# Context keys and values of two heads computed in the first stages and fetched in the attention

## The reference

```python
x = _layernorm(x + _L0_attn_ref(x, w1, w2, b2, sparse_mask))          # dense, masked, gelu
x = _layernorm(x + _L0_xattn_ref(x, ctx_4096, ctx_4096))              # autocorrelation
x = _layernorm(x + _L0_ffn_ref(x, base_W, router_W, lora_A, lora_B))  # routed low-rank
x = _layernorm(x + _L1_attn_ref(x, in_proj_w, ...))                   # state-space mixer
x = _layernorm(x + _L1_xattn_ref(x, ctx_4096, Wq, Wk, Wv, Wo, ...))   # cross attention
x = _layernorm(x + _L1_ffn_ref(x, gate, kernel, ...))                 # adapters
# in _L1_xattn_ref, with 32 query heads and 8 key heads of 128:
kv = jnp.concatenate([context, latents], axis=1)     # 128 context and 128 latent tokens
k = (kv @ Wk) ; v = (kv @ Wv)                        # then rms_norm of q and k, softmax, @ v, @ Wo
```

## Time and profile before

| | |
|---|---|
| median of 3 runs | 2551.83 us (2551.8 to 2552.94) |
| profiled execution, its own time | 2551.84 us |
| its span | 2550.1 us |
| TensorE busy | 2477.9 us, 97% |
| VectorE busy | 1866.3 us, 73% |
| ScalarE busy | 1122.6 us, 44% |
| GpSimd busy | 1082.3 us, 42% |

### The profile page before, as it was taken

The page is one execution under the profiler, slowest core; times in us unless marked ns, Lnnn a source line. Parts: engine busy times, 40 slices in busy tenths (PEclk is TensorE's granted clock), DMA queues, the critical chain, the costliest instruction groups (busy, mean ns, idle before and its releaser), DMA issues. The chain is left out here.

```text
span 2550.1 us, 39113 instructions
## 1 busy us (share of the span) xinstructions
PE 2477.9 (97%) x14056; PEld 2033.2 (80%) x14056; DVE 1866.3 (73%) x2530; ACT 1122.6 (44%) x2660; POOL 1082.3 (42%) x890
## 2 busy tenths in 40 slices
PE   7989899999999999999999999899999999999999
PEld 4547788888888888888888887788888888888886
DVE  4877986886977968859869678656666666666675
ACT  2323343343443443433434433455656556555551
POOL 3012655645655655556566555632312223222123
PEclk8999999999999999999999999999999999999999
DMA  4000420321412303313213131110101001000100
GB/s 151 28 1 9 164 101 30 144 95 54 145 42 91 120 29 120 116 38 136 71 64 139 38 116 64 60 42 26 34 18 34 26 17 42 16 27 26 56 3 34
DMA packets 61554, 163.82 MB, mean 64 GB/s; under 512 B 8336, under 2 KB 8976, under 8 KB 52944
## 3 DMA queue, kind: packets, MB, share of 16 engines
q1 hardware_dynamic: 60144, 159.21, 18.2%
q10 hardware_dynamic: 1248, 2.36, 0.3%
HBM read 158.92 MB, written 2.62 MB: 63 GB/s over the span
## 5 line engine op out<-in xcount | busy, mean ns | idle before, releaser
L271 PE MATMUL pair<-XH,d_w_hi 128*128 128x512 f32 x1160 | 471.8, 407 | 2.8 <-DVE d_gated L1633 1.7
L272 PE MATMUL pair<-XL,d_w_hi 128*128 128x512 f32 x1160 | 460.3, 397 | 0.0
L273 PE MATMUL pair<-XH,d_w_lo 128*128 128x512 f32 x1160 | 459.7, 396 | 0.0
L1492 POOL TENSOR_TENSOR d_decay<-d_decay,d_cb 128x1024 f32<-128x1024 f32 x128 | 311.1, 2431 | 137.2 <-DVE d_decay L1610 137.2
L1610 DVE TENSOR_TENSOR_SCAN d_decay<-d_decay,m_delta 128x1024 f32<-128x1024 f32 x128 | 363.5, 2841 | 1.5 <-DVE d_dtg L1578 1.5
L1473 POOL TENSOR_TENSOR d_w_lo<-d_w,d_w_hi 128x512 fp32r<-128x512 f32 x144 | 188.6, 1312 | 268.1 <-ACT d_w_hi L1313 267.4
L271 PEld LDWEIGHTS pair<-XH,d_w_hi 128*128 128x128 f32 x1160 | 218.8, 189 | 60.1 <-issue 12.8
L1595 DVE SCALAR_TENSOR_TENSOR d_hs<-pair,d_conv,d_hs 128x1016 f32<-128x1016 f32 (+2 forms) x192 | 242.9, 1265 | 29.2 <-ACT d_hs L1338 24.7
L273 PEld LDWEIGHTS pair<-XH,d_w_lo 128*128 128x128 f32 x1160 | 218.7, 189 | 52.9
L272 PEld LDWEIGHTS pair<-XL,d_w_hi 128*128 128x128 f32 x1160 | 219.0, 189 | 47.1
L1497 POOL TENSOR_TENSOR d_gated_lo<-d_gated,d_gated_hi 128x512 fp32r<-128x512 f32 x128 | 173.4, 1357 | 159.1 <-ACT d_gated_hi L1357 159.1
(11 more groups left out here) (280 smaller groups left out, 6032.4 us busy)
## 6 DMA issues: line engine op xcount, KB each, us to landing
d_decay<-token_decays SPq DMA_DIRECT2D x64, 1024.0 KB, 4.9
d_w<-in_L_w_groups SPq DMA_DIRECT2D x144, 256.0 KB, 2.7
e_w<-in_L_w_heads SPq DMA_DIRECT2D x80, 256.0 KB, 2.7
d_wo<-in_L_wo_groups SPq DMA_DIRECT2D x64, 256.0 KB, 4.9
X<-in_x SPq DMA_DIRECT2D x8, 256.0 KB, 10.3
b_ctx<-in_ctx SPq DMA_DIRECT2D x8, 256.0 KB, 12.0
e_ctx<-in_ctx_t SPq DMA_DIRECT2D x4, 512.0 KB, 6.5
out<-X SPq DMA_DIRECT2D x8, 256.0 KB, 2.0
```

Source lines behind the costliest of these rows:

```text
L271: pe.matmul(out, wh, xh, start=first, stop=False)
L272: pe.matmul(out, wh, xl, start=False, stop=False)
L273: return pe.matmul(out, wl, xh, start=False, stop=last)
L1492: pool.tensor_tensor(r, r, GM_[:], ALU.mult).then_inc(q["scores"], 1)
```

## The change

A new class `KeysAhead` projects the context's keys and values of heads 2 and 5 before the attention, as eight items of two batches (24 matmuls of 256 columns each). Items 0 and 1 stand behind the last dense batch in block one, in banks 4 and 5; items 2 to 7 stand in the autocorrelation, in bank 3 that its correlation also uses: item 2 ahead of `spectra(2)`, items 3 to 7 around `turn_weights` of batches 0, 2, 3, 4 and 5, half before and half after. For that the context and the weights are fetched and split in block one (residuals of batches 4 to 7, and the weights of the second head, in block two), each item is copied out by ScalarE and stored to DRAM from SP. The weights of the mixer that SP loads there now wait for the autocorrelation's last output. `next_hi` and `next_lo` do two slices in batch 2 and two in batch 3. In the attention, the sixteen units of these heads leave the context matmuls out; ScalarE issues two DMAs of 64 KB one unit ahead, and the operations that read keys and values from the bank are split into a context and a latent part. The context is loaded and split again for the other heads, as before. Buffers are moved between areas accordingly, and some semaphores are merged (not shown).

```diff
...
                     sp.dma_start(nxt["CTX"][:, b, :], nxt["ctx"][b]).then_inc(next_in, 16)
+                keys.weights(sp, 0)
+                keys.context(sp)
                 sp.wait_ge(next_in, 16 * (1 + NB))
+                for i in range(2):
+                    keys.store(sp, i)
             @block.scalar
...
                         turned_hi(c, act, first, b + 4, x_bank(b))
+                    if b == 1:
+                        keys.w_hi(act, 0)
+                    if 2 <= b < 6:
+                        keys.c_hi(act, b - 2)
+                for i in range(2):
+                    keys.copy(act, i)
+                    for b in (2 * i + 4, 2 * i + 5):
+                        keys.c_hi(act, b)
             @block.gpsimd
...
                         norm_rstd(c, pool, s, b - 1)
+                    if b == 1:
+                        keys.w_lo(pool, 0)
+                    if 2 <= b < 6:
+                        keys.c_lo(pool, b - 2)
                 norm_rstd(c, pool, s, NB - 1)
...
                         turn_x(b + 4)
+                pe.wait_ge(first.lo, NB)
+                for i in range(2):
+                    for half in range(2):
+                        keys.project(pe, i, half)
...
         self.WT = at("weights_t", [P, D])
-        self.AV, self.BV = e.place("b_av", [P, D], F32, "decay"), e.place("b_bv", [P, D], F32, "decay", D)
-        self.PR = e.place("b_products", [P, 4, D], F32, "decay", 2 * D)
+        self.AV, self.BV = e.place("b_av", [P, D], F32, "w"), e.place("b_bv", [P, D], F32, "w", D)
+        self.PR = e.place("b_products", [P, 4, D], F32, "w", 2 * D)
         self.q = sems(c, "b_", "const qf_ready qf_copied kf_ready spectra corr_ready corr_copied max8 less8 "
...
             pe.wait_ge(q["corr_copied"], b)
+        if b >= 2:
+            pe.wait_ge(self.keys.q["copied"], 4 if b < 4 else b + 1)
         for j in range(4):
...
             act.activation(nxt["AH"][:], nxt["A"][:], ACT.Copy).then_inc(q["next_hi"], 1)
-        if b in (2, 3, 4, 5):
-            act.activation(nxt["WH"][:, b - 2, :], nxt["W"][:, b - 2, :], ACT.Copy).then_inc(q["next_hi"], 1)
+        for k in {2: (0, 1), 3: (2, 3)}.get(b, ()):
+            act.activation(nxt["WH"][:, k, :], nxt["W"][:, k, :], ACT.Copy).then_inc(q["next_hi"], 1)
     def next_lo(self, pool, b):
...
                                ALU.subtract).then_inc(q["next_lo"], 1)
-        if b in (2, 3, 4, 5):
-            pool.wait_ge(q["next_hi"], b)
-            pool.tensor_tensor(nxt["WL"][:, b - 2, :], nxt["W"][:, b - 2, :],
-                               nxt["WH"][:, b - 2, :].bitcast(F32), ALU.subtract).then_inc(q["next_lo"], 1)
+        for k in {2: (0, 1), 3: (2, 3)}.get(b, ()):
+            pool.wait_ge(q["next_hi"], k + 2)
+            pool.tensor_tensor(nxt["WL"][:, k, :], nxt["W"][:, k, :],
+                               nxt["WH"][:, k, :].bitcast(F32), ALU.subtract).then_inc(q["next_lo"], 1)
     def products_of_spectra(self, v, b):
...
+class KeysAhead:
+    HEADS = (2, 5)
+    ITEMS = 4 * 2
+    def __init__(self, c, e, a, st, raw):
+        held, c.sems = c.sems, []
+        self.c, self.e, self.w_heads = c, e, a["L1_w_heads"]
+        self.kept = c.nc.dram_tensor("context_keys", (len(self.HEADS), NB, P, 2 * HD), F32).ap()
+        self.WR = c.nc.alloc_sbuf_tensor_at("k_w", [P, 2, D], F32, offset=raw)
+        self.WH, self.WL = e.place("k_w_hi", [P, 2, KD, P], F32R, "hs"), e.place("k_w_lo", [P, 2, KD, P], F32R, "hs", 2 * D)
+        self.OUT = [e.place("k_out", [P, 2, 2 * HD], F32, "w", 8 * D), e.place("k_out_next", [P, 2, 2 * HD], F32, "w", 7 * D)]
+        self.q = sems(c, "k_", "w_in w_hi w_lo c_in c_hi c_lo ready copied stored")
+        self.sems, c.sems = c.sems, held
+    def slot(self, i):
+        return self.OUT[1 if i == 1 else 0]
+    def bank(self, i):
+        return self.c.bank[4 + i if i < 2 else 3]
+    def weights(self, sp, x):
+        if x:
+            sp.wait_ge(self.q["w_lo"], x)
+        for i in range(2):
+            sp.dma_start(self.WR[:, i, :], self.w_heads[self.HEADS[x], K_ITEM + i, :, :]).then_inc(self.q["w_in"], 16)
+    def context(self, sp):
+        for k in range(KD):
+            sp.dma_start(self.e.CR[:, k, :], self.e.ctx_t[k * P:(k + 1) * P, :]).then_inc(self.q["c_in"], 16)
+    def store(self, sp, i):
+        sp.wait_ge(self.q["copied"], i + 1)
+        sp.dma_start(self.kept[i // 4, 2 * (i % 4):2 * (i % 4) + 2, :, :].rearrange("b p n -> p b n"),
+                     self.slot(i)[:]).then_inc(self.q["stored"], 16)
+    def w_hi(self, act, x):
+        act.wait_ge(self.q["w_in"], 32 * (x + 1))
+        if x:
+            act.wait_ge(self.q["ready"], 4 * x)
+        act.activation(self.WH[:].rearrange("p i k n -> p i (k n)"), self.WR[:], ACT.Copy).then_inc(self.q["w_hi"], 1)
+    def c_hi(self, act, b):
+        if b == 0:
+            act.wait_ge(self.q["c_in"], 16 * KD)
+        t = slice(b * S, (b + 1) * S)
+        act.activation(self.e.CH[:, :, t], self.e.CR[:, :, t], ACT.Copy).then_inc(self.q["c_hi"], 1)
+    def copy(self, act, i):
+        act.wait_ge(self.q["ready"], i + 1)
+        if i >= 2:
+            act.wait_ge(self.q["stored"], 16 * i)
+        act.activation(self.slot(i)[:].rearrange("p b n -> p (b n)"), self.bank(i)[:, :], ACT.Copy)\
+           .then_inc(self.q["copied"], 1)
+    def w_lo(self, pool, x):
+        pool.wait_ge(self.q["w_hi"], x + 1)
+        pool.tensor_tensor(self.WL[:].rearrange("p i k n -> p i (k n)"), self.WR[:],
+                           self.WH[:].bitcast(F32).rearrange("p i k n -> p i (k n)"), ALU.subtract)\
+            .then_inc(self.q["w_lo"], 1)
+    def c_lo(self, pool, b):
+        t = slice(b * S, (b + 1) * S)
+        pool.wait_ge(self.q["c_hi"], b + 1)
+        pool.tensor_tensor(self.e.CL[:, :, t], self.e.CR[:, :, t], self.e.CH[:, :, t].bitcast(F32), ALU.subtract)\
+            .then_inc(self.q["c_lo"], 1)
+    def project(self, pe, i, half):
+        b = 2 * (i % 4) + half
+        t = slice(b * S, (b + 1) * S)
+        pe.wait_ge(self.q["w_lo"], i // 4 + 1)
+        pe.wait_ge(self.q["c_lo"], b + 1)
+        for k in range(KD):
+            last = three_pass(pe, self.bank(i)[:, half * 2 * HD:(half + 1) * 2 * HD], self.e.CH[:, k, t], self.e.CL[:, k, t],
+                              self.WH[:, :, k, :], self.WL[:, :, k, :], k == 0, k == KD - 1)
+        if half:
+            last.then_inc(self.q["ready"], 1)
...
             pe.wait_ge(self.behind.q["corr_copied"], NB)
+            pe.wait_ge(self.behind.keys.q["copied"], KeysAhead.ITEMS)
         elif b == 1:
...
                 sp.sem_inc(preset, 1)
+                keys.weights(sp, 1)
+                for i in range(2, keys.ITEMS):
+                    keys.store(sp, i)
                 steps.inputs(sp)
+                sp.wait_ge(auto.q["out_ready"], NB)
                 for i in range(5):
...
                 auto.values(pe, 0)
+                pe.wait_ge(auto.q["corr_copied"], 2)
+                keys.project(pe, 2, 0)
+                keys.project(pe, 2, 1)
                 auto.spectra(pe, 2)
                 for b in range(NB):
+                    item = {0: 3, 2: 4, 3: 5, 4: 6, 5: 7}.get(b)
+                    if item is not None:
+                        pe.wait_ge(auto.q["corr_copied"], b + 2)
+                        if b == 0:
+                            pe.wait_ge(keys.q["copied"], item)
+                        keys.project(pe, item, 0)
                     auto.turn_weights(pe, b)
+                    if item is not None:
+                        keys.project(pe, item, 1)
                     auto.transform(pe, b)
...
                 auto.spectrum(act, 2)
+                keys.copy(act, 2)
                 for b in range(NB):
                     auto.weights_turned(act, b)
+                    item = {0: 3, 2: 4, 3: 5, 4: 6, 5: 7}.get(b)
+                    if item is not None:
+                        keys.copy(act, item)
+                    if b == 0:
+                        keys.w_hi(act, 1)
                     if b + 2 < NB:
...
                 steps.constants(pool)
+                for b in range(4, NB):
+                    keys.c_lo(pool, b)
+                keys.w_lo(pool, 1)
                 for b in range(NB):
...
             return slice((n % NB) * S, (n % NB + 1) * S)
+        def kept(n):
+            return keys.HEADS.index(n // NB) if 0 <= n < U and n // NB in keys.HEADS else None
+        KEPT = sb("e_kept", [P, 2, HD])
+        kept_in = [c.sem(f"e_kept_in{i}") for i in range(2)]
+        kept_order = [n for n in range(U) if kept(n) is not None]
+        def sides(n, kv):
+            if kept(n) is None:
+                return [(slice(0, 2), side(KVB, kv))]
+            first = KEPT[:, n % 2:n % 2 + 1, :] if kv else KN[:, n % 2, 0:1, :]
+            return [(slice(0, 1), first), (slice(1, 2), side(KVB, kv)[:, 1:2, :])]
         def ahead(eng, sem, count):
...
```

(33 more changed lines are left out.)

47 lines of the change are left out of this document (25 added, 22 removed).

## The result

The changed kernel took 2537.66 us (median of 4 runs, 2535.89 to 2538.48) against 2551.82 for the kernel before on the same chip: ratio 0.9944, 95% interval 0.9926 to 0.9961. The forecast was 2538.4 with a range of 2531 to 2548. The profiled execution took 2538.48 around a span of 2536.6, so the span fell by 13.5 us from the 2550.1 before.

A forecast was written before the change was run, and what follows sets the result against it. TensorE was taken to bound the attention, and TensorE with VectorE to fill the autocorrelation. Attention -19.4, first stage +3.0 and autocorrelation +3.0 (+10.6 - 7.6) sum to -13.4: 2538.4 us, range 2531 to 2548.

The forecast's parts named there:

- Attention, -19.4 forecast: Attention: context matmuls removed from sixteen units give -22.9 us, ScalarE's overrun in weight-splitting units costs +3.5.
- the loop of ScalarE: Kept attention units: ScalarE's work with DMA issues and weight splits takes 11.7 to 11.8 us, 0.4 over TensorE's 11.38.
- The split in `sides`: Attention: value copy, value residual and key scaling split in two, about 0.1 to 0.2 us each beyond the single form.
- First stage, +3.0 forecast: Block one: added residuals lengthen GpSimd's batches to about 3.7 us, +3.0 us; the added matmuls fall in a TensorE hole, free.
- Rival (c): First stage: back-to-back GpSimd operations hold VectorE's normalisation, some 1.2 us more for each of four batches, 2543 us; chance 0.07.
- Autocorrelation, items +10.6 forecast: Autocorrelation: six items of 24 matmuls mostly lengthen TensorE's work, +0.9 for the first and 1.95 for each of five others.
- The 0.9 of item 2: Autocorrelation, ahead of the first batch: partly inside TensorE's 1.66 us wait, so turned weights +0.9 us instead of 2.8.
- Autocorrelation, the move, -7.6 forecast: Autocorrelation: residuals `c_w_lo` 2 and 3 done earlier remove `base(0)`'s wait and its lower clock, gain 7.6 us.
- Rival (b): Autocorrelation: `base(0)` does not move, or its gain is lost to the wait for batches 6 and 7; 2546 us; chance 0.11.
- Rival (a): ScalarE's issues and GpSimd's residuals are covered, and first spectra win a microsecond from shorter TensorE idle; 2532 us; chance 0.16.
- (d): Attention: ScalarE's loop keeps kept units at the old period, removed matmuls become waits at `score`; 2558 us; joint chance 0.08.
- (e): Attention: fetched keys come late or the context matmuls are not skipped; 2558 us; chance 0.08 shared with the preceding rival.

The follow-up runs named there:

- experiment 4: The changed kernel with the two fetches of a kept unit issued by SyncE instead of ScalarE: 2537.79 us, ratio 0.9945.
- experiment 5: The changed kernel with GpSimd's residuals of the weights of heads 3 and 6 over 16 of 512 columns (output less exact or wrong): 2533.51 us.
- experiment 7: The changed kernel with GpSimd's power of q ahead of the two weight residuals at a unit's end: 2542.12 us, ratio 0.9966.
- experiment 8: The changed kernel with GpSimd's head-weight residuals moved into the next unit, behind its `k_norm`: 2538.86 us, ratio 0.995.
- experiment 6: The changed kernel with GpSimd's key and value weight residuals waiting until `k_norm` of their unit is done: 2535.4 us.
- experiment 2: The kernel before with only the base weight slices' copies and residuals moved, two a batch in batches 2 and 3: 2543.88 us, ratio 0.9967.
- experiment 11: The changed kernel run once more, word for word: 2536.66 us, ratio 0.9943.
- experiment 9: The changed kernel with block one's weights split early: 2535.85 us; also with query/output residuals behind next `k_norm`, key/value ones behind the negated maximum: 2532.03 us.
- experiment 1: The changed kernel with `next_hi` and `next_lo` back to one slice a batch in batches 2 to 5: 2546.87 us, ratio 0.9982.
- experiment 3: The changed kernel with items 3 to 7 at 2 matmuls instead of 24 (their keys and values wrong): 2530.76 us.

## Why the prediction was right, and where it was not

**The total**: 2538.4 forecast, 2537.66 measured. The large terms hold one by one, below; the part that varies from run to run could have moved it by a microsecond or two either way. That the sum came out within 0.8 us is in part luck.

**Attention, -19.4 forecast, -18.8 measured.** The removed matmuls gave 1.42 a unit (1.43). The waits cost 93.1 - 91.14 = 1.96 a head, 3.9 in all (3.5). The size held, by luck; the mechanism did not. The step that failed is the loop of ScalarE, "adding 0.94 and 0.1 gives 10.7 ... in the units in which two weight tiles are also split ... 11.7 to 11.8: 0.4 over". The period of 11.75 matched it, and for the wrong reason: the issues cost nothing (experiment 4), and what closes in a weight unit is a loop through GpSimd's queue, residuals, powers, `k_norm` (experiments 5, 7 and 8). Five units a head were charged with 0.4 each; in fact the residuals lie in four, and these cost 0, 0.29, 0.36 and 1.33. The last one I had put with the others, and 0.98 of its 1.33 (12.72 less 11.74) came because `k_norm`, newly reading SBUF instead of a bank, ran beside a residual (experiment 6). Without that the two heads would have lost 1.9 us, not 3.9. The split in `sides` looked harmless and was priced at 0.1 us; it gave VectorE two SBUF inputs. The Trainium skill, SBUF — State Buffer, "Who interferes with whom", says just this: a VectorE instruction with two SBUF inputs contends with a GpSimd instruction that reads SBUF. The traces agree (1.38 and 0.29 us, 0.96 and 0.16 us). I had drawn on that section for the normalisation only and not asked which operands the change moves from bank to SBUF.

**First stage, +3.0 forecast, +2.35 measured.** GpSimd pays, as worked through; the term was mis-sized because a batch with a residual mostly takes 3.53 us, not 3.7 (its own terms, 1.29 + 0.48 + 0.57 + 1.3, add to 3.64). The granted clock from 25 to 31 us was 0.72 in both traces; where it was 1.00, the same stretch is 32.34 us in the kernel of experiment 2 and 34.68 in that of experiment 11, again 2.34 apart. Taking away the 1.06 of the early weights (experiment 9) leaves 1.3 for the context residuals. Rival (c), several residuals in a row holding a normalisation, would have given +7.8 (3.0 and four times 1.2) and didn't come.

**Autocorrelation, items +10.6 forecast.** From the first correlation to batch 0's turned weights +2.38 (0.9 + 1.4 = 2.3), to batch 5's +7.65, and for the last half +0.62 in experiment 1, where `base(0)` waits as before (21.49 us from batch 5's turned weights to batch 6's against 20.87): 10.65. Experiment 3 gives 1.95 an item, as forecast. The 0.9 of item 2 doesn't follow from its own numbers (2.8 less 1.66 is 1.1), but the trace has it: 2.38 less 1.43.

**Autocorrelation, the move, -7.6 forecast**: -7.58 alone (experiment 2), 7.7 when taken back (experiment 1). Rival (b) is out.

**What wasn't foreseen** is the run-to-run part: start of the sparse-weight matmuls 24.14 to 25.78 us, -1.55 where the clock of 25 to 31 us is full, 6.85 to 8.30 us from first spectrum to first correlation, 1.12 to 2.08 us for the last transform's first two matmuls, and 99.4 to 101.6 us for head 0 of the attention where no edit touches it (99.48 before and 99.45 after, so no part of the difference). The base of 2551.84 was taken as if all of these stood still. Rival (a) counted on the third of these getting a microsecond shorter with TensorE's idle time; the traces give no such order (8.30 us behind 4.54 us of idle in the changed kernel, 7.60 behind 7.93 before), though the two shortest, 6.85 and 7.01, are those behind the shortest idle, 3.5 us with the early weights. What decides these clocks stays open.

Rivals (d) and (e) are out: the plain kept units take 11.39 us with no wait.

## What to carry to other kernels

Before a bank read is turned into an SBUF read, look which GpSimd operation runs beside it: a VectorE operation of 0.29 us became one of 1.38, in a unit with no slack. Where an engine's own queue carries both long background work and short links of the critical chain (here two residuals ahead of two powers), put the background behind the link and behind the neighbour's contended operations; it cost two waits and gave 3.9 us. Behind the link alone it took 0.6 us from every ordinary head (experiment 8), so look at the heads that weren't changed too. And look at each edit by itself: more than half of this gain was a reordering of two small copies and residuals that the new matmuls did not need.

## What the runs showed of the hardware that I had not expected

Two DMA issues on ScalarE's queue (0.33 and 0.46 us) run while the engine executes an activation of 0.68 us, and moving them to SyncE changed a head of 93.1 us by nothing.

The contention does not scale with the size of the VectorE operation: one of four columns was held for 0.8 us, until the GpSimd operation beside it ended (at 1946.81, by which a residual of 1.3 us that began at 1945.50 is over).

One program, run again, differed by 2.0 us in its first 70 us (first correlation at 70.21 and 68.22), mostly through the granted clock, while its units of head 2 repeated to 0.01 us; single spans of this kernel can't be compared to better than that without cutting them into stretches. The Trainium skill, TensorE: Matmul & The Clock Gate, "What's actually happening", calls the slow start of one kernel run-variable. No run here shows that at the start itself, where both traces of the changed kernel have a granted clock of 1.00 up to 25 us; what varied are the later places named above.
